# First attention of a two-layer model: per-head q and k stacks assembled by on-chip transfers instead of engine copies, pairs of heads written out

## What is computed

```python
# layer 0, xn = layernorm(x); 16 heads of 64, rope on q and k, causal
q, k, v = split_heads(xn @ Wq), split_heads(xn @ Wk), split_heads(xn @ Wv)
q, k = apply_rope(q), apply_rope(k)
sim = einsum('bid,bjd->bij', q, k) * 64 ** -0.5      # masked to the causal half
s = einsum('bij,bjd->bid', softmax(sim), v)          # heads joined, @ Wo + bo
g = silu(down(silu(gate(xn)) * up(xn)))
x = x + s * g
# layer 1: the same frame, 16 heads of 16 and eight experts
```

## Time and profile before

| | us |
|---|---|
| median of 3 runs | 2184.87 |
| lowest and highest | 2182.67, 2185.92 |
| the profiled execution, its own time | 2188.42 |
| its span, first to last instruction | 2186.7 |
| PE busy | 1986.1 (91% of the span) |
| DVE busy | 1535.2 (70%) |
| ACT busy | 1394.3 (64%) |
| POOL busy | 675.9 (31%) |
| DMA over the span | 35 GB/s |

### The profile page before, as it was taken

The page is one execution under the profiler, slowest core; times in us unless marked ns, Lnnn a source line. Parts: engine busy times, 40 slices in busy tenths (PEclk is TensorE's granted clock), DMA queues, the critical chain, the costliest instruction groups (busy, mean ns, idle before and its releaser), DMA issues. The chain is left out here.

```text
span 2186.7 us, 41413 instructions
## 1 busy us (share of the span) xinstructions
PE 1986.1 (91%) x12160; PEld 1479.5 (68%) x12160; DVE 1535.2 (70%) x3292; ACT 1394.3 (64%) x3261; POOL 675.9 (31%) x1032
## 2 busy tenths in 40 slices
PE   2999999999999999999999969995799999999997
PEld 1777768768768777777687658885556566656653
DVE  5786885885876867868868853442577777777773
ACT  3675675775665756756757745552477776776774
POOL 0353442443443443434434413333000111011012
PEclk9999999999999999999999979998699999999999
DMA  6000000000000000000000055222100110111001
GB/s 222 1 0 11 10 0 20 0 0 20 0 0 20 0 0 20 0 10 10 0 10 1 0 182 233 102 98 70 36 20 1 49 48 0 48 48 46 2 29 39
DMA packets 52360, 76.87 MB, mean 35 GB/s; under 512 B 1856, under 2 KB 42688, under 8 KB 51776
## 3 DMA queue, kind: packets, MB, share of 16 engines
q1 hardware_dynamic: 51744, 75.05, 9.9%
q10 hardware_dynamic: 544, 1.05, 0.2%
HBM read 55.12 MB, written 20.97 MB: 35 GB/s over the span
## 5 line engine op out<-in xcount | busy, mean ns | idle before, releaser
L1539 DVE TENSOR_REDUCE nm<-ps 128x1 f32<-128x512 f32 x512 | 337.1, 687 | 116.0 <-PE ps L1398 112.2
L826 POOL TENSOR_SCALAR pr<-pr,rinv 128x128 f32<-128x128 f32 (+3 forms) x512 | 262.8, 532 | 409.0 <-DVE rinv L700 409.0
L1650 ACT ACTIVATE pt<-pst 128x512 f32<-128x512 f32 x512 | 296.0, 602 | 143.0 <-PE pst L1406 141.8
L557 ACT ACTIVATE pr<-sc,nmax 128x128 f32<-128x128 f32 (+3 forms) x512 | 263.2, 529 | 88.2 <-DVE nmax L689 88.2
L832 POOL TENSOR_TENSOR qk<-ra,rb 128x256 f32<-128x256 f32 x256 | 195.3, 774 | 275.8 <-DVE rb L713 236.5
L1398 PE MATMUL ps<-kb,qb 96*128 96x512 f32 x512 | 239.6, 470 | 12.1 <-DVE nm L1539 9.6
L404 PE MATMUL w<-ident,pr 128*128 128x128 f32 x1280 | 194.2, 286 | 41.0 <-DVE qs L720 25.5
L689 DVE TENSOR_REDUCE nmax<-sc 128x1 f32<-128x128 f32 (+3 forms) x512 | 216.3, 482 | 19.9 <-PE sc L392 19.6
L390 PE MATMUL sc<-k,qs 128*128 128x256 f32 (+2 forms) x512 | 212.3, 416 | 12.4 <-DVE k L727 11.2
L1406 PE MATMUL pst<-qb,kb 128*128 128x512 f32 x512 | 208.1, 408 | 6.7 <-ACT pt L1650 3.6
L1398 PEld LDWEIGHTS ps<-kb,qb 96*128 96x128 f32 x512 | 98.6, 193 | 144.1 <-DVE nm L1539 95.5
(11 more groups left out here) (207 smaller groups left out, 4982.1 us busy)
## 6 DMA issues: line engine op xcount, KB each, us to landing
raw<-in_w SPq DMA_DIRECT2D x16, 704.0 KB, 5.6
raw<-in_w SPq DMA_DIRECT2D x8, 640.0 KB, 5.1
xa<-in_x SPq DMA_DIRECT2D x2, 2048.0 KB, 13.8
x<-in_x SPq DMA_DIRECT2D x8, 512.0 KB, 3.5
x_scratch<-x SPq DMA_DIRECT2D x8, 512.0 KB, 3.5
xt_hi_scratch<-xt_hi SPq DMA_DIRECT2D x1, 4096.0 KB, 13.5
xt_lo_scratch<-xt_lo SPq DMA_DIRECT2D x1, 4096.0 KB, 23.3
gate_scratch<-go SPq DMA_DIRECT2D x32, 128.0 KB
```

Of the source, the lines that this page charges most:

```text
L557: act.activation(pr[:, h, SOFF[i]:SOFF[i] + (i + 1) * P], sc[:, bank, at:at + (i + 1) * P], ACT.Exp, bias=nmax[:, h, i:i + 1], accum_out=r ...
L826: pool.tensor_scalar(p, p, rinv[:, h, i:i + 1], 1.0, ALU.mult, ALU.mult).then_inc(scaled, 1)
L1539: dve.tensor_reduce(nm[:, g % 2, i, h:h + 1], ps[:, i % 2, :], AXX, ALU.max, negate=True).then_inc(max_done, 1)
L1650: act.activation(pt[:, g % 2, h, i, :], pst[:, i % 2, :], ACT.Exp).then_inc(exp_done, 1)
```

## The change

Both heads' q and k are split over 128 partitions at once: ACT casts q high and k high into `qh` and `kh`, DVE subtracts to `ql` and `kl`. SP then assembles the stacks of a pair from them by twelve transfers from SBUF to SBUF, each 64 partitions by 512 floats (128 KB), on two semaphores, one for each head. `scores(n, h)` waits until the six transfers of its head have landed. Everything that SP does is written out: 64 stacks, the loads and the stores in one list. The banks that `turn_p` writes are free when `ql` and `kl` are done. The two half products of rope become one, which reads the two halves in reverse order; the table has its two sine parts swapped for it. The inner loops over pairs 1 to 5 are written out on PE, ACT and DVE (POOL keeps its loop), and with a fixed place in the ring `weigh` reads `v_ring` itself; `v_cur` is gone. A row's SP work is now: store x1 of the row before, stack of pair 0, load of the next x, stacks of pairs 1 to 7.

```diff
     ang = (np.arange(T, dtype=np.float32)[:, None] * inv[None, :]).astype(np.float32).astype(np.float64)
-    t = np.stack([np.cos(ang), np.sin(ang), -np.sin(ang)], 1).astype(np.float32)
...
             def _(sp):
+                def stack(n):
+
+                    sp.wait_ge(qk_hi_done, 2 * n + 1)
+                    for h in range(2):
+                        sp.dma_start(qs[HALF[0], h, :].bitcast(F32), qh[HALF[h], :].bitcast(F32)).then_inc(stacked[h], 16)
+                    sp.wait_ge(qk_hi_done, 2 * n + 2)
+                    for h in range(2):
+                        sp.dma_start(k1[HALF[0], h, :].bitcast(F32), kh[HALF[h], :].bitcast(F32)).then_inc(stacked[h], 16)
+                        sp.dma_start(k2[HALF[1], h, :].bitcast(F32), kh[HALF[h], :].bitcast(F32)).then_inc(stacked[h], 16)
+                    sp.wait_ge(qk_lo_done, 2 * n + 1)
+                    for h in range(2):
+                        sp.dma_start(qs[HALF[1], h, :].bitcast(F32), ql[HALF[h], :].bitcast(F32)).then_inc(stacked[h], 16)
+                    sp.wait_ge(qk_lo_done, 2 * n + 2)
+                    for h in range(2):
+                        sp.dma_start(k1[HALF[1], h, :].bitcast(F32), kl[HALF[h], :].bitcast(F32)).then_inc(stacked[h], 16)
+                        sp.dma_start(k2[HALF[0], h, :].bitcast(F32), kl[HALF[h], :].bitcast(F32)).then_inc(stacked[h], 16)
...
+                def row(b, first=False, last=False):
+                    if not first:
+                        store_x1(b - 1)
+                    stack(NP0 * b)
+                    if not last:
+                        load_x(b + 1)
+                    for hp in range(1, NP0):
+                        stack(NP0 * b + hp)
...
                 def scores(n, h):
-                    pe.wait_ge(hi_copied, 2 * n + h + 1)
-                    pe.wait_ge(lo_copied, 2 * n + h + 1)
+                    pe.wait_ge(stacked[h], 96 * n + 96)
...
-                def weigh(n):
+                def weigh(n, hp):
 
                     pe.wait_ge(pt_a_copied, 3 * n + 3)
                     pe.wait_ge(pt_b_copied, 3 * n + 3)
-                    pe.wait_ge(v_cur_done, n + 1)
+                    pe.wait_ge(v_done, NT * n + NT)
                     pe.wait_ge(o_lo_done, n + 1)
                     for kt in range(NT):
                         for h in range(2):
-                            mm = pe.matmul(po[h * D0:(h + 1) * D0, kt * P:T], v_cur[:, kt, h * D0:(h + 1) * D0],
+                            mm = pe.matmul(po[h * D0:(h + 1) * D0, kt * P:T], v_ring[:, hp % 4 * NT + kt, h * D0:(h + 1) * D0],
                                            pt[:, h, PTOFF[kt]:PTOFF[kt] + T - kt * P], start=(kt == 0), stop=(kt == NT - 1))
...
                     if first:
-                        pe.wait_ge(stack_lo, 4 * n + 4)
+                        pe.wait_ge(qk_lo_done, 2 * n + 2)
                     scores(n, 0)
...
-                        weigh(n - 1)
+                        weigh(n - 1, hp - 1)
                     for j in (2, 0, 1):
                         if j < 2 and turn:
-                            pe.wait_ge(stack_lo, 4 * (n + 1) + 3 + j)
+                            pe.wait_ge(qk_lo_done, 2 * (n + 1) + 1 + j)
...
-                    with pe.Fori(1, NP0 - 2) as hp:
+                    for hp in range(1, NP0 - 2):
                         pair(b, hp)
```

On ACT:

```diff
                     act.wait_ge(proj_done, NT * n + i + 1)
-                    act.copy(v_ring[:, bass.ds(hp % 4 * NT + i, 1), :].rearrange("p o d -> p (o d)"), w[:, bank, 4 * D0:PC0]).then_inc(v_done, 1)
-
-                def take_qk(n, h, banks=w):
-
-                    own, other = HALF[h], HALF[1 - h]
-                    act.wait_ge(qk_turned, 2 * n + 2)
-                    if h == 1:
-                        act.wait_ge(stack_lo, 4 * n + 1)
-                    act.copy(qs[own, h, :], banks[own, 1, :]).then_inc(stack_hi, 1)
-                    act.wait_ge(qk_turned, 2 * n + 3)
-                    if h == 1:
-                        act.wait_ge(stack_lo, 4 * n + 2)
-                    act.copy(k1[own, h, :], banks[own, 2, :]).then_inc(stack_hi, 1)
-
-                def copy_half(n, h):
-
-                    act.wait_ge(stack_hi, 4 * n + 2 * h + 2)
-                    act.copy(k2[HALF[1 - h], h, :], k1[HALF[h], h, :].bitcast(F32)).then_inc(hi_copied, 1)
+                    act.copy(v_ring[:, hp % 4 * NT + i, :], w[:, bank, 4 * D0:PC0]).then_inc(v_done, 1)
+
+                def take_qk(n, banks=w):
+
+                    for j, hi in enumerate((qh, kh)):
+                        act.wait_ge(qk_turned, 2 * n + 2 + j)
+                        act.copy(hi[:], banks[:, 1 + j, :]).then_inc(qk_hi_done, 1)
...
-                    if not first:
-                        pass_v(n - 1, hp - 1)
                     if turn:
-                        take_qk(n + 1, 0)
+                        take_qk(n + 1)
                     if slot == "project" or slot == "next_row":
                         take_v(*ahead, 2, SLOT[2])
                     exps(n, 1)
-                    if turn:
-                        take_qk(n + 1, 1)
                     if slot == "project" or slot == "next_row":
                         take_v(*ahead, 3, SLOT[3])
-                    if turn:
-                        copy_half(n + 1, 0)
-                    if turn:
-                        copy_half(n + 1, 1)
...
-                    take_qk(n, 0, sc)
-                    for i in range(2):
+                    take_qk(n, sc)
+                    for i in range(NT):
                         take_v(n + 1, 1, i, FOUR[i])
-                    take_qk(n, 1, sc)
-                    for i in range(2, NT):
-                        take_v(n + 1, 1, i, FOUR[i])
-                    copy_half(n, 0)
-                    copy_half(n, 1)
...
-                    pass_v(b * NP0 + NP0 - 1, NP0 - 1)
```

On DVE:

```diff
-                    dve.tensor_tensor(r[:, :, 0, :], src[:, :, 1, :],
-                                      c.rope[:, i, 2, :].unsqueeze(1).to_broadcast([P, 4, D0 // 2]), ALU.mult)
-                    dve.tensor_tensor(r[:, :, 1, :], src[:, :, 0, :],
-                                      c.rope[:, i, 1, :].unsqueeze(1).to_broadcast([P, 4, D0 // 2]), ALU.mult).then_inc(rope_mult, 1)
-
-                def take_qk(n, h, banks=w):
-
-                    own, other = HALF[h], HALF[1 - h]
-                    dve.wait_ge(stack_hi, 4 * n + 2 * h + 1)
-                    dve.tensor_tensor(qs[other, h, :], banks[own, 1, :], qs[own, h, :].bitcast(F32), ALU.subtract).then_inc(stack_lo, 1)
-                    dve.wait_ge(stack_hi, 4 * n + 2 * h + 2)
-                    dve.tensor_tensor(k2[own, h, :], banks[own, 2, :], k1[own, h, :].bitcast(F32), ALU.subtract).then_inc(stack_lo, 1)
-
-                def copy_half(n, h):
-
-                    dve.wait_ge(stack_lo, 4 * n + 2 * h + 2)
-                    dve.tensor_copy(k1[HALF[1 - h], h, :], k2[HALF[h], h, :].bitcast(F32)).then_inc(lo_copied, 1)
+                    dve.tensor_tensor(r, src[:, :, ::-1, :], c.rope[:, i, 1:3, :].unsqueeze(1).to_broadcast([P, 4, 2, D0 // 2]),
+                                      ALU.mult).then_inc(rope_mult, 1)
+
+                def take_qk(n, banks=w):
+
+                    for j, (hi, lo) in enumerate(((qh, ql), (kh, kl))):
+                        dve.wait_ge(qk_hi_done, 2 * n + 1 + j)
+                        dve.tensor_tensor(lo[:], banks[:, 1 + j, :], hi[:].bitcast(F32), ALU.subtract).then_inc(qk_lo_done, 1)
...
                     if turn:
-                        take_qk(n + 1, 0)
+                        take_qk(n + 1)
                     if slot == "project" or slot == "next_row":
                         rope(ahead, 2, SLOT[2])
                     invert(n, 1)
-                    if turn:
-                        take_qk(n + 1, 1)
-                        copy_half(n + 1, 0)
-                        copy_half(n + 1, 1)
...
-                    take_qk(n, 0, sc)
-                    for i in range(2):
+                    take_qk(n, sc)
+                    for i in range(NT):
                         rope(n + 1, i, FOUR[i])
-                    take_qk(n, 1, sc)
-                    for i in range(2, NT):
-                        rope(n + 1, i, FOUR[i])
-                    copy_half(n, 0)
-                    copy_half(n, 1)
```

More of the change, by code:

```diff
@@ L54, in rope_tables @@
     ang = (np.arange(T, dtype=np.float32)[:, None] * inv[None, :]).astype(np.float32).astype(np.float64)
-    t = np.stack([np.cos(ang), np.sin(ang), -np.sin(ang)], 1).astype(np.float32)
+    t = np.stack([np.cos(ang), -np.sin(ang), np.sin(ang)], 1).astype(np.float32)
     return np.ascontiguousarray(t.reshape(NT, P, 3, D0 // 2).transpose(1, 0, 2, 3))
@@ L229, in layer0 @@
         qk = t.sb("qk", [P, NT, 4 * D0])
-        qs = t.sb("qs", [P, 2, T], F32R)
-        k1 = t.sb("k1", [P, 2, T], F32R)
-        k2 = t.sb("k2", [P, 2, T], F32R)
+        qh, ql, kh, kl = (t.sb(n, [P, T], F32R) for n in ("qh", "ql", "kh", "kl"))
```

(20 more changed lines are left out.)

12 lines of the change are left out of this document (8 added, 4 removed).

## The result

| | before | after |
|---|---|---|
| median of the runs, us | 2185.39 (4 runs, 2182.67 to 2189.0) | 2399.56 (4 runs, 2397.68 to 2404.19) |
| ratio, 95% interval | | 1.098 (1.096 to 1.1004) |
| span of the profiled execution, us | 2186.7 | 2397.7 |
| TensorE's mean granted clock | 0.972 | 0.919 |

The kernel became slower by 214 us. The forecast was 2256 us, +71, with a range up to 2338: the sign was right, the size was a third of what came.

What follows compares the result with a forecast made beforehand. TensorE was taken to bound the first layer. Late stacks +45 us and half clock +22 and +4 made +71, from 2188.4 to 2260 profiled, 2256 us as median; range for 8 in 10: 2152 to 2338.

Steps and rivals of the forecast that it cites:

- place 10 of the queue: SP's queue: head 0's six transfers stand at 1, 3, 4, 7, 9 and 10, so the tenth decides when scores start.
- the low parts no hindrance: Both subtractions are over some 1.5 us after `qh`, while SP is still busy with its first four transfers.
- a launch of the chain right after the cast: SP wakes 0.1 us after ACT's cast of `qh` ends, at 404.05 in the steady pair.
- the issue step: SP's queue: 0.53 us per transfer, 4.77 us to the tenth issue, bounds 3.87 and 5.67.
- the landing: A 128 KB transfer lands 2.1 us after issue, between 1.8 and 2.4; 6.87 us after SP's wake with the issues.
- the sum: Late stacks at seven places a row, +0.68 us per steady pair: 5.7 us a row, 45 us for eight rows.
- the high end: Step 0.63 and landing 2.4: stack after 8.07 us, 112 us of waits, 48 for the clock, 2346 us.
- rival 1: Bandwidth: ten queued transfers share a path at 200 GB/s, 0.65 us each; 2336 us; chance 0.22 shared with the high end.
- the clock: Half clock on TensorE after idling: every second steady wait at 1.1 us, 22 us, plus 4 in pair 6.
- the relief and the written-out code: About 2.9 us off DVE per pair, fewer ACT casts, no `v_cur` copy, written-out pairs; costed at zero, covered by TensorE's queue.
- the "issue" idle at the start of a row: Sign that longer loop bodies make instruction loading visible; costed at zero.
- Rival 2: Faster: issue 0.37, landing 1.8, the stack beats the old chain; 2167 us; chance 0.28 with everything below the balance.

Runs made afterwards that it cites:

- e1: The change with SP's twelve transfers sorted by head, head 0's six first, so its last is sixth instead of tenth; 2148.2 us, ratio 0.983.
- e5: The change with head 1's six transfers first, so head 0's last is twelfth in SP's queue instead of tenth; 2486.8 us, ratio 1.137.
- e4: The change with each transfer cut to 128 of 512 columns (32 KB) from the second stack on; 2349.3 us, ratio 1.074.
- e3: The change with 24 extra transposes on TensorE before each wait for head 0's stack, from pair 1 on; 2315.9 us, ratio 1.060.
- e9: e7 with SP's ten transfers cut to 32 KB from the second stack on, ScalarE's two staying 128 KB; 2092.4 us, ratio 0.957.
- e2: The kernel before plus single rope product, written-out pairs and `weigh` reading `v_ring`, stacks still copied by engines; 2184.1 us, ratio 0.9987.
- e7: e1 with head 0's first two transfers issued by ScalarE instead of SP; 2166.3 us, ratio 0.9926.

## Why the prediction was right or wrong

**Right: the place, and what decides there.** 56 waits for a transfer of head 0, decided by place 10 of the queue; the low parts no hindrance; the turns of probabilities down to 1.31 us (1.26 forecast); a launch of the chain right after the cast (0.02 us; 0.1 forecast). e1, e5 and the change differ in the order of the queue alone.

**Wrong: the issue step, 0.53 us.** It is 0.64: 5.64 us to the tenth issue instead of 4.77. I took the middle between a load over 128 partitions, 0.43, and the one transfer with 64 partitions, up to 0.63, with the argument that the latter always follows another one closely. That is just what these twelve do: the first in an idle queue takes 0.46 to issue (e1, below), those behind it 0.60. The row nearest in circumstances, close behind another transfer, was the one to take, not the middle. That being close behind is not the whole reason stands in the same rows: the load of `xa` follows another load at once and took 0.41.

A stretch of SP's timeline in e1:

```profile
462.33 0.46 SPq L309 DMA_DIRECT2D qs<-qh  x1
462.83 0.60 SPq L313 DMA_DIRECT2D k<-kh  x1
463.47 0.60 SPq L314 DMA_DIRECT2D k<-kh  x1
```

**Wrong: the landing, 2.1 us.** 2.3 by its own row, 2.47 until the scores start. The Trainium skill's formula in "DMA: Bandwidth & Descriptors", section "Anatomy of one DMA", had given 2.3 as an estimate, and the trace agrees with it, although the page fits its formula to transfers issued by GpSimd; for e4's 32 KB it gives 2.1, where the trace has 1.9. Issue and landing together make the stack of a steady pair 1.84 us late (467.03 - 457.67 = 9.36 after the turn, 7.52 before) where +0.68 was forecast. Over all 56 waits the time from turn to scores grew from 7.40 to 9.62 us on average, 124 us in all, where the sum had 45. The steady pair above is the high end's chain almost to the digit (8.07 forecast, 8.11 measured), so the case that came had been given a small part of the 0.22 it shared with rival 1.

**Wrong: the clock, 26 us.** e3 puts it at 84 net and some 100 gross. I had let the half clock follow every second steady wait and priced it at 1.1 us, from a pair where it began 1.1 us before the scores, in the turns, and covered only their first 2.1 us. Here it follows all 56 waits, begins about with the scores (0.4 us after them in the pair above, between 4.0 before and 1.1 after in the others) and stands until 3.3 to 6.6 us after their start, into the turns and beyond: from the scores to the next turn of q and k the steady pair above takes 8.36 us, e3 6.79. That is 1.57 us a time, and more in the ten of 32 steady pairs where it lasts longer. This is the largest part of why the time lies above even the high end, 2346, which had counted 48 us for the clock; the waits, 124 us against its 112, are the smaller part.

**Priced at nothing: the relief and the written-out code.** A steady pair became 17.72 - 14.74 = 2.98 us longer, not 1.84 + 1.57 = 3.41; the 0.43 between them is what the relief of the engines gave back. e9 shows all of it: its steady pairs have no wait and take 13.20, not the 13.9 that I had expected. Against that stand the crossings, 1.9 us a row in e2, with the "issue" idle at the start of a row that the prediction had named as the sign of it, and issues held up beside instruction loads. In the pair at 436 us the sixth issue took 1.76 us:

```profile
441.49 0.69 SPq L312 DMA_DIRECT2D k<-kh  x1
442.22 1.76 SPq L313 DMA_DIRECT2D k<-kh  x1
...
448.41 0.58 PE L415 MATMUL sc<-k,qs 128*128 128x256 f32 x1 [6.02 <-DMA k<-kl]
```

and of the DMA engines' time from 442.2 to 442.6 a load of instructions took 22%:

```profile
q8 instruction: 1, 0.02, 22.0%
```

Of SP's 768 stack issues 21 took over 0.8 us, 14 us over the usual together. 20 of them are among the 35 issues with a load of that queue begun from 0.45 us before their start to their end; of the 733 others one is as long. In e3 90 issues meet a load and 48 of them are long, in e4 18 and 9. That the load is the cause was not tested by a run that moves the loads alone. Taken together, 124 us of waits and some 100 of the clock are 14 us more than the 210 that the layer lost: by about that the relief outweighs the rest, an estimate that is no better than the 100 in it.

**Rival 1, bandwidth,** was wrong as the bound of this change, since e4's issues kept their pace with a quarter of the bytes. Its number was nearly right: 0.65 us for a transfer at some 200 GB/s, where the share gives 0.59. The limit stands 0.05 us behind the issue step, and e7 ran into it. **Rival 2, faster,** had its chain wrong (no issue of 0.37 in a row), yet the gain it speaks of exists: e1 gets it from the order alone.

What stays open: why an issue takes 0.60 us behind another one here. Partitions and bytes do not matter; a transfer that neither starts nor ends in SBUF was not tried in such a row.

## What to carry to other kernels

When a chain of transfers replaces work on engines, price the queue: place of the last transfer that is needed, times the issue step of a row that stands close behind another, plus the landing; then sort the queue by who needs what first, which here turned 1.098 into 0.983 (0.988 the second time). A wait on TensorE costs its length and then the matmuls behind it at the lower clock, here 1.57 us for 2.65 us of wait. A second queue helps only while the DMA engines' share leaves room: read it in the stretch where the first queue issues.

## What the runs showed of the hardware

- An issue from SP of an SBUF to SBUF transfer took 0.46 us in an idle queue and 0.60 us (a step of 0.64) behind another one, whether it moved 32 or 128 KB, over 64 or 128 partitions.
- Transfers over 64 partitions moved 204 GB/s at a DMA share of 0.91, over 128 partitions 199 at 0.59; two issuers together reached 226 at 0.96, and landings rose from 2.4 to 3.2 us.
- 24 transposes that nobody reads, in each wait, made the kernel 84 us faster than the same kernel without them; time at the lower clock in the first layer fell from some 300 us to 41.
- Of SP's issues that met an instruction load (queue q8), about half took over 0.8 us (20 of 35 in the change, up to 2.0 us) instead of 0.60; of the others 1 of 733.
- ScalarE's second issue in e7 took up to 1.74 us (0.61 in the median) and held its casts and copies up for as long.
